# Attention row sums computed by TensorE as further rows, image sum moved to GpSimd, tail moved by two slots

## What is computed

```python
scores = jnp.einsum('bhnqd,bhnkd->bhnqk', qw, kw) * scale + pos_bias[None, :, None]
probs = jax.nn.softmax(scores, axis=-1)
ow = jnp.einsum('bhnqk,bhnkd->bhnqd', probs, vw)
merged = jnp.zeros(...).at[:, :, flat].add(ow.reshape(B, H, -1, D))   # windows of 128, step 64, and a last one
merged = merged / counts
return merged_to_rows @ Wo + bo
```

## Time and profile before

| | us, or share |
|---|---|
| median of 3 runs | 1357.6 |
| lowest, highest | 1352.97, 1358.94 |
| the profiled execution | 1365.91 |
| its span, first to last instruction | 1364.1 |
| its mean granted TensorE clock | 0.925 of full |
| TensorE, VectorE, ScalarE, GpSimd busy, share of the span | 87%, 67%, 57%, 42% |

### The profile page before, as it was taken

The page is one execution under the profiler, slowest core; times in us unless marked ns, Lnnn a source line. Parts: engine busy times, 40 slices in busy tenths (PEclk is TensorE's granted clock), DMA queues, the critical chain, the costliest instruction groups (busy, mean ns, idle before and its releaser), DMA issues.

```text
span 1364.1 us, 34942 instructions
## 1 busy us (share of the span) xinstructions
PE 1180.1 (87%) x10190; PEld 949.8 (70%) x10191; DVE 913.4 (67%) x4211; ACT 779.0 (57%) x3176; POOL 571.8 (42%) x718
## 2 busy tenths in 40 slices
PE   1376889988998899889888764999999999999996
PEld 1254566666665666566666543999999999999995
DVE  4484998998989998999897754444444444444442
ACT  0295998999999999999999951111111111111110
POOL 5432466456545654565455332322223322222322
PEclk9687999888989898898889975999999999999998
DMA  3793564356436643664366126233233333333232
GB/s 113 150 238 84 117 149 90 89 129 145 85 90 137 136 92 92 137 131 89 93 125 133 33 68 184 40 48 50 46 48 48 46 47 50 46 46 50 46 47 31
DMA packets 98400, 123.35 MB, mean 90 GB/s; under 512 B 15544, under 2 KB 87416, under 8 KB 95192
## 3 DMA queue, kind: packets, MB, share of 16 engines
q1 hardware_dynamic: 75880, 89.96, 29.9%
q0 software_dynamic: 18576, 24.47, 11.2%
q10 hardware_dynamic: 3808, 7.34, 2.0%
HBM read 69.35 MB, written 46.07 MB: 85 GB/s over the span
## 4 chain that ended last, share of the span: by engine, by line
PE 67%; ACT 13%; issue 7%; DVE 4%; DMA 4%; POOL 1%; SPq 1%; ACTq 0%; DVEq 0%; another core or an unknown queue 0%; POOLq 0%
PE s_bank L1178 12%; PE t_bank L1178 12%; PE o_bank L1193 11%; ACT probs L628 10%; PE t_bank L1050 8%; PE m_bank L1114 5%; PE o_bank L1073 5%; PE s_bank L1036 4%; PE m_bank L1021 3%; PE m_bank L1014 3%; DMA qk_parts<-parts_flat 2%; DVE probs L765 2%; PE o_bank L1082 2%; ACT probsT L642 2%; PE m_bank L1167 1%
## 5 line engine op out<-in xcount | busy, mean ns | idle before, releaser
L628 ACT ACTIVATE probs<-probs,neg_max 128x128 f32<-128x128 f32 x1280 | 498.1, 403 | 7.5 <-issue 3.7
L765 DVE CUSTOM_DVE_ANT_0 probs<-s_bank,nbias 128x128 f32<-128x128 f32 x1280 | 291.8, 284 | 35.9 <-PE s_bank L1036 33.9
L628 ACT ACTIVATION_READ_ACCUMULATOR probs<-probs,neg_max 128x1 f32 x1280 | 260.4, 203 | 0.0
L1050 PE MATMUL t_bank<-ident,probs 128*128 128x128 f32 x1280 | 220.6, 300 | 39.6 <-ACT probs L628 39.2
L687 ACT ACTIVATE v_all<-s_bank 128x512 f32<-128x512 f32 x91 | 54.4, 598 | 287.7 <-PE s_bank L1178 267.8
L1050 PEld LDWEIGHTS t_bank<-ident,probs 128*128 128x128 f32 x1280 | 150.8, 154 | 54.0 <-ACT probs L628 50.9
L1036 PE MATMUL s_bank<-stacks 96*128 96x128 bf16 x1280 | 137.4, 234 | 49.4 <-DMA stacks<-qk_parts 32.3
L1193 PE MATMUL o_bank<-stacks,v_all 128*128 x728 | 172.7, 380 | 1.4 <-issue 1.2
L642 ACT ACTIVATE probsT<-t_bank 128x512 f32<-128x512 f32 x240 | 141.9, 591 | 51.1 <-PE t_bank L1050 49.7
L1036 PEld LDWEIGHTS s_bank<-stacks 96*128 96x128 bf16 x1280 | 94.2, 105 | 110.5 <-issue 39.1
L1073 PE MATMUL o_bank<-probsT,v_all 128*32 128x128 f32 x2560 | 146.0, 303 | 19.0 <-ACT probsT L642 12.6
(11 more groups left out here) (158 smaller groups left out, 2023.8 us busy)
## 6 DMA issues: line engine op xcount, KB each, us to landing
stacks<-qk_parts SPq DMA_DIRECT2D x192, 166.5 KB
qk_parts<-parts_flat SPq DMA_DIRECT2D x192, 83.2 KB
nbias<-expert_slots SPq DMA_DIRECT2D x91, 129.0 KB
w_sb<-in_L_ffn_w_dram ACTq DMA_DIRECT2D x14, 512.0 KB
v_all<-v_all SPq DMA_DIRECT2D x64, 96.0 KB, 3.2
x_here<-in_x_dram SPq DMA_DIRECT2D x16, 256.0 KB, 3.0
out_dram<-h_res SPq DMA_DIRECT2D x16, 256.0 KB
stacks<-in_L_ffn_w_dram SPq DMA_DIRECT2D x8, 512.0 KB
```

Source lines behind the costliest of these rows:

```text
L628: ins = act.activation(seg, seg, ACT.Exp, bias=neg_max[:, r, i:i + 1], scale=-1.0, accum_out=row_sum[:, (par + v) % 2, h:h + 1])
L765: ins = dve.tensor_tensor_reduce(probs[:, r, i * WIN:(i + 1) * WIN], s_bank[:, k % 2, i * WIN:(i + 1) * WIN], nbias[:, h, :], 1.0, BIG, AL ...
L1050: mm = pe.transpose(t_bank[:, (k - 3) % 2, i * WIN:(i + 1) * WIN], probs[:, r, i * WIN:(i + 1) * WIN], ident[:, :])
```

## The change

Four things change.

1. **Row sums.** `v_all` is filled with ones in place of zeros, so that the second half of each product's 32 rows is the sum of the exponentials. Each group gets its own part of `o_bank` (no accumulation over two groups). The exponentials lose their row sum.
2. **Normalisation.** ScalarE copies all 512 columns of a window (`raw`), TensorE transposes them back into query layout (four transposes), VectorE takes two reciprocals of the sums from PSUM and makes two products into `ctx_q`, TensorE transposes that (two), ScalarE copies it to `head_out`. GpSimd's sum into the context comes three slots later. The copy to `probsT` that VectorE makes is now that of group 1 of a window (`DVE_G`).
3. **Image.** The sum of the two differences and the clip go to GpSimd, slot 6 in place of 7. The moments of the first layer norm move from slot 11 to 8.
4. **Places.** Output projection 6, 7 to 8, 9; residual 8 to 10; second moments 10 to 11; V projection all in 11; split parts' middle one slot later; prefix a slot earlier and payload one later. Prefix and gate write to `m_bank` instead of `o_bank`. GpSimd's sum into `h_res` waits for the normalised rows of the next batch.

The diff, cut:

```diff
-            pool.memset(v_all[:, :], 0.0).then_inc(zeroed, 1)
+            pool.memset(v_all[:, :], 1.0).then_inc(zeroed, 1)
...
+                    if inp and k == 6:
+                        pool.wait_ge(conv_step, b2 * 3 + 2)
+                        pool.tensor_tensor(diag[:, :, :], diag[:, :, :], anti[:, :, :], ALU.add).then_inc(conv_step, 1)
...
+                        pool.tensor_scalar(h_in[par][:, 0:2, :], diag[:, :, :], 1.0, 0.0, ALU.min, ALU.max)\
+                            .then_inc(image_ready, 1)
...
                     if proj and k == 18:
...
+                        if inp:
+                            pool.wait_ge(xn_ready, b2 * 3 + 3)
...
-                            ins = act.activation(seg, seg, ACT.Exp, bias=neg_max[:, r, i:i + 1], scale=-1.0,
-                                                 accum_out=row_sum[:, (par + v) % 2, h:h + 1])
+                            ins = act.activation(seg, seg, ACT.Exp, bias=neg_max[:, r, i:i + 1], scale=-1.0)
...
                     v = (k - 4) // NG
...
-                        act.wait_ge(weightT_done, b * NW + v + 1)
...
-                        act.activation(weightT[:, :], o_bank[:, (par + v) % 2, C * WIN:2 * C * WIN], ACT.Copy)\
-                            .then_inc(weightT_ready, 1)
+                        act.wait_ge(pv_done, wv * NG + NG)
...
+                        act.activation(raw[:, :], o_bank[:, (par + v) % 2, :], ACT.Copy).then_inc(raw_ready, 1)
+                    v = (k - 7) // NG
...
+                        act.wait_ge(headT_done, wv + 1)
...
+                        act.activation(head_out[:, vp, :], o_bank[:, vp, 0:C * WIN], ACT.Copy).then_inc(head_ready, 1)
...
-                        dve.reciprocal(inv_sum[:, vp, :], row_sum[:, vp, :]).then_inc(inv_ready, 1)
...
-                        dve.tensor_reduce(weight[:, vp, :, :],
-                                          inv_sum[:, vp, :].unsqueeze(2).unsqueeze(3).to_broadcast([P, H, HD, 1]),
-                                          AX.X, ALU.add)\
-                            .then_inc(weight_ready, 1)
...
-                        dve.tensor_tensor(head_out[:, vp, :], o_bank[:, vp, 0:C * WIN], weightT[:, :], ALU.mult)\
-                            .then_inc(head_ready, 1)
+                    v = (k - 6) // NG
...
+                        dve.wait_ge(rawT_done, wv + 1)
...
+                        for a in range(2):
+                            dve.reciprocal(inv[:, :, :, a:a + 1], sums[a]).then_inc(inv_ready, 1)
...
+                            dve.tensor_tensor(heads[:, :, :, a, :], src[:, :, :, a * HD:(a + 1) * HD],
+                                              inv[:, :, :, a:a + 1].to_broadcast([P, 2, GH, HD]), ALU.mult)\
+                                .then_inc(ctx_q_ready, 1)
...
-                    if inp and k == 7:
-                        dve.wait_ge(conv_step, b2 * 3 + 2)
-                        dve.tensor_tensor(diag[:, :, :], diag[:, :, :], anti[:, :, :], ALU.add).then_inc(conv_step, 1)
...
-                        dve.tensor_scalar(h_in[par][:, 0:2, :], diag[:, :, :], 1.0, 0.0, ALU.min, ALU.max)\
-                            .then_inc(image_ready, 1)
...
+                        pe.wait_ge(raw_ready, wv + 1)
+                        for g in range(NG):
+                            mm = pe.transpose(o_bank[:, vp, g * WIN:(g + 1) * WIN], raw[:, g * WIN:(g + 1) * WIN],
+                                              ident[:, :])
+                        mm.then_inc(rawT_done, 1)
...
+                        pe.wait_ge(ctx_q_ready, wv * 2 + 2)
+                        for c in range(C):
+                            mm = pe.transpose(o_bank[:, vp, c * WIN:(c + 1) * WIN], ctx_q[:, c * P:(c + 1) * P],
+                                              ident[:, :])
+                        mm.then_inc(headT_done, 1)
```

More of the change, by code:

```diff
@@ L566, in step @@
                         scatter(1, 2)
-                    if (tail or inp) and k == 11:
+                    if (tail or inp) and k == 12:
                         if tail:
@@ L636, in step @@
                     g = (k - 2) % NG
-                    if g != 3 and ((k >= 2 and att) or (k < 2 and tail)):
+                    if g != DVE_G and ((k >= 2 and att) or (k < 2 and tail)):
                         n = b * G + (k - 2)
@@ L1116, in step @@
                         mm.then_inc(qk_done, 1)
-                    if tail and k == 6:
+                    if tail and k == 8:
                         pe.wait_ge(ctx_added, b0 * NW + NW)
@@ L1124, in step @@
                         out_proj(0)
-                    if tail and k == 7:
+                    if tail and k == 9:
                         out_proj(1)
```

160 lines of the change are left out of this document (83 added, 77 removed).

## The result

| | before | after |
|---|---|---|
| median, us | 1357.5 (4 runs) | 1393.5 (4 runs) |
| lowest, highest | 1352.97, 1358.94 | 1392.55, 1395.82 |
| ratio | | 1.027, 95% interval 1.025 to 1.030 |
| span of the profiled execution | 1364.1 | 1390.1 |
| period of a batch | 45.4 | 47.7 |

The forecast was 1312 (1275 to 1345). The loop alone carries the difference: the memset of the context answers the earlier trace rows, and (792.6 - 125.3)/14 is 47.7 us a batch, 2.3 more than before, where the forecast had 3.1 less. 2.3 x 15 = 35 us, and the medians differ by 36.

A forecast was written before the change was run, and what follows sets the result against it. Three almost full engines were taken to bound it: TensorE in A, ScalarE and VectorE in B. A 25.4 and B 17.3 made 42.7 against 45.8, -3.1 us a batch, about -45 in all: 1312 us, range 1275 to 1345.

The forecast's parts named there:

- The moves: VectorE's row copy, prefix, payload, moments and split parts change slots: same instructions, nothing saved, counted as zero.
- What is late next there is the transpose wait: VectorE in B: its wait for ScalarE's weights goes; the wait for transposes, 1.4 us a batch, stays.
- The wait for raw: TensorE's raw transposes wait for ScalarE: 0.5 us where the slot before has no projection; +0.6 taken for A.
- sign of being wrong: TensorE's raw transposes waiting for ScalarE, or head transposes for VectorE, above 0.7 us a window would refute the forecast.
- A: Stretch of a batch, TensorE's slots 1 to 11, with the projections: TensorE works 23.8 of 24.7 us; forecast 25.4.
- The added transposes: TensorE, net four more a window: 2.2 us a batch, 0.9 of it in A, the rest in B.
- B: Stretch of a batch, slots 12 to 0, 21.1 us: ScalarE (19.9) and VectorE (19.3) are full; forecast 17.3.
- The contention at xn: GpSimd's sum into h_res no longer runs beside VectorE's three normalisations: 1.9 us a batch off, in B.
- The exponentials: ScalarE's step without a row sum falls from 0.39 to 0.2 us: 15 us off its batch; it leaves the path.
- conv work: The image's sum and clip, 2.8 us on VectorE in A, go to GpSimd: 0.8 us a batch off the path.
- first rival: Only TensorE and VectorE totals bind, 40.7 and 37.8 us a batch: -5.1 a batch, 1283 us, chance 0.2.
- third rival: TensorE's two new waits stall it: 1379 us at 1.0 us a window, 1422 if every window stalls; chance 0.08.

The follow-up runs named there:

- a_rf_vsplit: a_rawfirst with the last third of the V projection issued one slot later, in slot 12: 1348.7 us.
- a_rf_g3l: a_rawfirst with VectorE's copy of probsT for group 3, placed behind the window's reciprocals and products: 1345.8 us, 1346.8 when run again.
- a_rawfirst: The changed kernel with ScalarE's copy of raw issued ahead of the slot's four exponentials: 1375.1 us.
- b_g1: The kernel before with VectorE copying probsT for group 1 and ScalarE for group 3: 1387.7 us, ratio 1.040.
- b_noacc: The kernel before with exponentials that keep no row sum, the sums a constant written once: 1318.9 us, ratio 0.970.
- b_moretr: The kernel before with four more transposes a window and no new wait: 1380.2 us, ratio 1.014.
- b_reswait: The kernel before with GpSimd's sum into h_res waiting for the three normalisations of xn: 1362.1 us, ratio 0.999.
- a_convdve: The changed kernel with the image's sum and clip back on VectorE, in slot 7: 1392.4 us.
- b_conv: b_reswait plus the image's sum and clip on GpSimd, in slot 6: 1353.3 us, ratio 0.991.

## Why the prediction was wrong

**The sum over one batch.** Forecast -3.1 us, measured +2.3, so 5.4 us to find.

**The moves: the step that failed.** The prediction said of VectorE's row copy that it "goes to group 1 of a window" with "nothing saved", at zero. It priced the instruction and not what stands behind it. By a_rf_vsplit and a_rf_g3l against a_rawfirst (46.8 to 44.6) the copy behind the whole V projection costs 2.2 us a batch. In the kernel before the copy's move alone costs 1.8 (b_g1, 47.2 against 45.4; 3.4 by its own session, 1387.7 against 1336.0). Moving either the copy or a third of the projection gives the 2.2 back, and moving both gives no more (1345.8 and 1348.7, 1347.5 together). The order of the instructions showed it before any run: the V projection all in slot 11, and the copy there needing transposes of slot 12. "What is late next there is the transpose wait (1.4 a batch), which stays" is the sentence that should have been worked out; it became 5.5 (71.9/13).

**The wait for raw: right place, short by some.** The estimate of 0.5 us a window rested on exponentials at 0.2 us. With 0.29 it is 0.9, the copy of the heads (0.38) stands there too, and the trace shows 0.8 on average and up to 1.1 in 53 windows. That is above the 0.7 us a window that the forecast named as its sign of being wrong. The 0.6 in the sum counted slots of A alone. Undone, it gives back 1.0 us a batch.

**The added transposes.** The number was about right (2.2 us a batch): TensorE is busy 40.8 us a batch in the changed kernel and 38.2 in b_noacc, which lacks them, both at a clock of 0.97. But only the 0.9 in A was counted, "the rest in B, where there is room". b_moretr puts 1.3 us on the path, so 0.4 more.

**The contention at xn: right mechanism, wrong effect.** Three normalisations do take 1.1 us, but -1.9 a batch became -0.2 (b_reswait). It was taken from a stretch that the forecast itself called ScalarE's.

**The exponentials.** The step is 0.29 and not 0.2. ScalarE needs 38.6 us a batch; the prediction had 38 for that case. The gain alone was 2.9 at most, in b_noacc, and 1.1 by the kernel before's lower level.

**Adding it up.** Against the forecast, a batch: copy 2.2; raw 0.4 (the 1.0 that its repair gave back less the 0.6 that was counted); contention 1.7; transposes 0.4 (1.3 less the 0.9 that was counted); conv work 0.8, since a_convdve shows no gain from it here; and up to 1.0 to the good for the exponentials, 2.9 in b_noacc against the 1.5 and 0.4 in the sum. Together 4.5 of the 5.4 looked for. The 0.9 left is assigned to nothing: the other moves (output projection, residual, moments, prefix) and the waits of the head transposes were not run by themselves, and with the exponentials at their lower 1.1 the same sum gives 6.3. The terms were measured in different kernels and overlap, so the sum orders them by size and proves none.

**Right in detail.** The first rival's TensorE total (40.7 forecast, 40.8 measured) and VectorE's (37.8 and 37.3), the clock nearer to full, no scores waiting for stacks, no output projection waiting for GpSimd. VectorE's new four instructions take 0.72 us from 581.34 to 582.06, forecast 1.0. The sum on GpSimd took 1.29 us (forecast 1.10): the Trainium skill (GPSIMD Engine Reference, Engine selection) says that two-input work is about twice as slow there; the estimate from it and VectorE's free 0.69, 1.4, was nearer.

**The rival.** The sign was the third rival's, "the round trip stalls TensorE", with a chance of 0.08 and a price of 1379 at 1.0 us a window. It has less than half of the mechanism: undoing the wait for `raw` gives back 18 us, and undoing VectorE's copy behind the V projection 26 to 29 us more, which no rival named. The word against it, "both partners work a slot ahead", held for neither: ScalarE has four exponentials ahead, VectorE a projection.

## What to carry to other kernels

When an in-order engine's instruction moves to another slot, write down which instruction of the other engine it needs, what long work stands ahead of that one, and what stands behind the moved one on its own engine: the price is that lump, not the instruction. Busy totals said that this change would gain, and those of TensorE and VectorE were right within 0.5 us; with three engines busy 78 to 86% of the loop, the period was set by who stands behind whom. In this kernel it paid to put the copy that must wait last in its slot (a_rf_g3l), and the copy that others wait for first (a_rawfirst). And where a kernel shows two levels of the granted clock, a gain against one level alone says little.

## What was not expected of the hardware

Leaving out the accumulator output shortened the exponential's step from 0.39 to 0.29 us, though its own duration stayed at 398 ns (403 in the earlier trace rows). GpSimd clipped 512 columns in 0.76 us (b_conv), VectorE in 1.52 while GpSimd worked beside it. And the kernel before moved by 2% from session to session (1336 to 1366), with its mean granted clock at 0.95 to 0.96 or at 0.92 to 0.94, while the changed kernel and a_rf_g3l, each in two sessions, stayed within 0.1%.
